# x turned in blocks by VectorE and through DRAM, and the carried sum added on GpSimd, in a Mamba-2 layer

## The reference

```
proj = layernorm(x) @ in_proj_w.T          # gate 8192 | hBC 8192 + 2*8*128 | dt 128
hBC  = silu(causal_conv4(hBC) + conv_b)    # hs (128 heads x 64), B, C (8 groups x 128)
dt   = clip(softplus(dt + dt_bias))
xch  = hs * dt                             # per token and head
Y_diag = (C B^T * L) xch                   # inside a chunk of 128 tokens
states = B^T (decay * xch)                 # one per chunk
new_states = states carried from chunk to chunk
Y_off  = C prev_state * exp(A_cum)         # from the chunks before
y    = Y_diag + Y_off + hs * D
g    = y * silu(gate); normed over groups of 1024 features; * norm_w
x    = x + g @ out_proj_w.T
```

## Time and profile before

| | us |
|---|---|
| median of 3 runs | 1605.14 |
| lowest and highest run | 1604.95, 1605.45 |
| the profiled execution, its span | 1605.0 |
| PE busy | 1583.5 (99%) |
| DVE busy | 1264.2 (79%) |
| ACT busy | 1163.1 (72%) |
| POOL busy | 700.7 (44%) |

### The profile page before, as it was taken

One profiled execution on the slowest core, in us unless ns is written; L12 is line 12 of the kernel. 1 busy time (PEld: TensorE's weight loads), 2 busy tenths in 40 slices (PEclk: granted clock), 3 DMA queues, 4 the chain that ended last, 5 costly groups with the idle time before them and its releaser, 6 DMA issues.

```text
span 1605.0 us, 26714 instructions
## 1 busy us (share of the span) xinstructions
PE 1583.5 (99%) x9576; PEld 1346.1 (84%) x9576; DVE 1264.2 (79%) x1984; ACT 1163.1 (72%) x2027; POOL 700.7 (44%) x535
## 2 busy tenths in 40 slices
PE   7899999999999999999999999999999999999998
PEld 5688888888888888888888888888888888888887
DVE  6687777877778777887778877787877878788787
ACT  5887667776777677777687766777677767777753
POOL 2155444453444454354453544445344445435550
PEclk9999999999999999999999999999999999999999
DMA  4542322332323233332232232233232323223211
GB/s 151 192 145 86 122 89 83 112 112 73 112 97 114 73 109 95 98 106 92 99 108 97 86 122 89 83 112 112 73 112 99 113 73 109 99 92 112 93 44 53
DMA packets 86916, 162.37 MB, mean 101 GB/s; under 512 B 23040, under 2 KB 39424, under 8 KB 86528
## 3 DMA queue, kind: packets, MB, share of 16 engines
q1 hardware_dynamic: 86784, 160.66, 30.8%
HBM read 154.84 MB, written 5.77 MB: 100 GB/s over the span
## 4 chain that ended last, share of the span: by engine, by line
PE 97%; DVE 1%; ACT 1%; issue 0%; DMA 0%; SPq 0%; DVEq 0%; ACTq 0%
PE g_bank L778 10%; PE g_bank L780 9%; PE g_bank L779 9%; PE d_bank L797 7%; PE x_bank L778 7%; PE x_bank L780 7%; PE x_bank L779 7%; PE head_bank L786 5%; PE head_bank L804 5%; PE x_bank L836 4%; PE x_bank L837 4%; PE x_bank L835 4%; PE d_bank L837 4%; PE d_bank L835 4%; PE d_bank L836 4%; PE head_bank L812 3%
## 5 line engine op out<-in xcount | busy, mean ns | idle before, releaser
L1448 POOL TENSOR_TENSOR w_low<-raw,w_high 128x512 fp32r<-128x512 f32 x139 | 179.8, 1294 | 553.5 <-ACT w_high L1011 553.5
L1199 DVE SCALAR_TENSOR_TENSOR hs<-x_bank,cols,hs 128x1022 f32<-128x1022 f32 x189 | 241.6, 1278 | 129.7 <-ACT hs L1033 127.5
L1021 ACT ACTIVATE scores<-scores,tables 128x128 f32<-128x128 f32 x1024 | 312.4, 391 | 0.0
L1462 POOL TENSOR_TENSOR y<-y,gate 128x512 f32<-128x512 f32 x128 | 185.4, 1467 | 198.8 <-DVE y L1268 198.8
L1033 ACT ACTIVATE hs<-x_bank,cols 128x1024 f32<-128x1024 f32 x63 | 75.9, 1204 | 269.9 <-PE x_bank L780 269.9
L778 PE MATMUL g_bank<-x_high,w_high 128*128 128x512 f32 x624 | 250.8, 402 | 0.0
L779 PE MATMUL g_bank<-x_low,w_high 128*128 128x512 f32 x624 | 243.2, 390 | 0.0
L780 PE MATMUL g_bank<-x_high,w_low 128*128 128x512 f32 x624 | 243.1, 390 | 0.0
L778 PE MATMUL x_bank<-x_high,w_high 128*128 128x512 f32 x504 | 196.3, 390 | 0.1
L780 PE MATMUL x_bank<-x_high,w_low 128*128 128x512 f32 x504 | 196.1, 389 | 0.0
L779 PE MATMUL x_bank<-x_low,w_high 128*128 128x512 f32 x504 | 196.1, 389 | 0.0
(11 more groups left out here) (211 smaller groups left out, 3433.3 us busy)
## 6 DMA issues: line engine op xcount, KB each, us to landing
scores<-sums_dram SPq DMA_DIRECT2D x128, 512.0 KB, 4.8
raw<-w_in SPq DMA_DIRECT2D x144, 256.0 KB, 2.9
grown_rows<-grown_dram SPq DMA_DIRECT2D x256, 96.0 KB, 2.8
out_raw<-w_out SPq DMA_DIRECT2D x64, 256.0 KB, 3.4
mixed<-x SPq DMA_DIRECT2D x8, 256.0 KB, 5.1
out<-mixed SPq DMA_DIRECT2D x8, 256.0 KB, 2.0
table_dram<-table SPq DMA_DIRECT2D x2, 768.0 KB, 5.3
tables<-table_dram SPq DMA_DIRECT2D x30, 48.0 KB, 2.7
```

The lines of the kernel that those rows point to most:

```text
L1021: op = s.activation(at, at, ACT.Relu, bias=col[:, r, c:c + 1], scale=-1.0)
L1199: v.scalar_tensor_tensor(out=hs[:, q % 2, :, i:], in0=x_bank[:, :, 0:SEQ - i], scalar=cols[:, q, TAPS - 1 - i:TAPS - i], in1=hs[:, q % 2, ...
L1448: pool.tensor_tensor(w_low[:, slot], raw[:, slot], w_high[:, slot].bitcast(F32), ALU.subtract)\
L1462: pool.tensor_tensor(y[:, b], y[:, b], gate[:, q % 2, b], ALU.mult).then_inc(y_ready, 1)
```

## The change

Hs of a unit is no longer turned by TensorE (only that of the very first unit is). DVE transposes it in blocks of 32x32 (`turn_blocks`), SP stores the blocks to DRAM (`store_blocks`, one DMA of 512 KB) and loads them back in four DMAs of 128 KB, each to 32 partitions, in pieces of 1 KB (`load_heads`), so that tokens lie on the partitions. `to_heads` reads this buffer instead of `head_bank`, with dt doubled in the tables (four kinds instead of three), and it has moved behind the two scores. `add_carry` has moved from DVE to GpSimd, ahead of each `gated`. In SP's queue the store stands before `load_grown` and the loads behind it. `states` now waits for `carry_scaled` of the unit before, as `turn_hs` did. The split bias has no buffers of its own any more and uses parts of x_low and x_high, so its copy waits until all projections are done.

The diff, without signatures and allocations:

```diff
             def table_of(i):
-                s.activation(table[:, b, :, kind].rearrange("p g (h c) -> p c g h", c=CHUNKS), ..., ACT.Copy)
+                if kind == 0:
+                    twice = table[:, b, :, 0:2].rearrange("p g k (h z c) -> p z c g (k h)", z=2, c=CHUNKS)
+                    s.activation(twice[:, 0], src, ACT.Copy)
+                    s.activation(twice[:, 1], src, ACT.Copy).then_inc(table_ready, 1)
...
+            def store_blocks(k):
+                sp.wait_ge(blocks_ready, k)
+                reached(sp, heads_in, 16 * QUARTERS * (k - 2))
+                sp.dma_start(blocks_dram[k % 2], blocks[:].rearrange("p j n f -> p (j n f)"))\
+                  .then_inc(blocks_stored, 16)
+
+            def load_heads(k):
+                sp.wait_ge(blocks_stored, 16 * k)
+                turned_blocks = blocks_dram[k % 2].rearrange("(q t) (j n) -> j t q n", t=BLOCK, j=QUARTERS)
+                for i in range(QUARTERS):
+                    sp.dma_start(blocks[i * BLOCK:(i + 1) * BLOCK].rearrange("p q n f -> p q (n f)"),
+                                 turned_blocks[i]).then_inc(heads_in, 16)
...
                     if ahead:
+                        store_blocks(ahead[2])
                         for b in range(BATCH):
                             load_grown(ahead[2], b)
+                        load_heads(ahead[2])
...
             def states(k, b):
                 pe.wait_ge(xdecay_ready, BATCH * k + b + 1)
+                reached(pe, carry_scaled, BATCH * (k - 1) + b + 1)
...
-                    if ahead:
-                        for b in range(BATCH):
-                            turn_hs(k + 1, (j + 1) % 2, b)
...
+            def turn_blocks(k, i):
+                v.wait_ge(hs_ready, k + 1)
+                reached(v, blocks_stored, 16 * (k - 1))
+                v.transpose(blocks[:], hs[:, i].rearrange("p b (c j t) -> p j (b c) t", j=QUARTERS, t=BLOCK))\
+                 .then_inc(blocks_ready, 1)
...
             def to_heads(g, q, k, b):
...
+                else:
+                    v.wait_ge(heads_in, 16 * QUARTERS * k)
+                    v.tensor_tensor(xdt[:, b].rearrange("p c r (h f) -> p (r h) c f", f=BLOCK),
+                                    blocks[:, :, CHUNKS * b:CHUNKS * (b + 1)],
+                                    dt_of(b, q).unsqueeze(3).to_broadcast([P, QUARTERS, CHUNKS, BLOCK]), ALU.mult)\
+                     .then_inc(xdt_ready, 1)
...
-                    for b in range(BATCH):
-                        to_heads(g, j, k, b)
+                    if k == 0:
+                        for b in range(BATCH):
+                            to_heads(g, j, k, b)
...
                     if scores_here:
                         score(g, j, k, 1)
+                    if k > 0:
+                        for b in range(BATCH):
+                            to_heads(g, j, k, b)
...
                         skip(j, k)
+                        turn_blocks(k + 1, (j + 1) % 2)
                         for b in range(BATCH):
                             carry_part(k, b)
-                        for b in range(BATCH):
-                            add_carry(k, b)
...
         @block.gpsimd
+            def add_carry(k, b):
+                u = BATCH * k + b
+                pool.wait_ge(skip_added, k + 1)
+                pool.wait_ge(carry_scaled, u + 1)
+                pool.tensor_tensor(y[:, b, P:], y[:, b, P:], grown[:, b].rearrange("p c l -> p (c l)"), ALU.add)\
+                    .then_inc(y_sum, 1)
...
                     for b in range(BATCH):
+                        add_carry(k, b)
                         gated(j, k, b)
...
-        bias_high, bias_low = sb("bias_high", [P, HID], F32R), sb("bias_low", [P, HID], F32R)
+        bias_high, bias_low = x_low[:, 1, 0], x_high[:, 1, 0]
...
+                        s.wait_ge(projected, BATCH * TILES)
                         s.activation(bias_high[:], bias_row, ACT.Copy).then_inc(bias_high_ready, 1)
```

More of the change, by code:

```diff
@@ L21 @@
 PAIR = P // HEAD_DIM
+BLOCK = 32
+KINDS = 4
+QUARTERS = P // BLOCK
 GH = HEADS // GROUPS
@@ L158, in prologue @@
         sums, grown = big("head_sums"), big("head_grown")
-        table = sb("table", [P, BATCH, 2 * GROUPS, 3, GH // 2 * CHUNKS])
+        table = sb("table", [P, BATCH, 2 * GROUPS, KINDS, GH // 2 * CHUNKS])
         la, lb = sb("la", [P, ER, HID]), sb("lb", [P, ER, HID])
@@ L400, in table_of @@
                 s.wait_ge(table_turned, i + 1)
-                s.activation(table[:, b, :, kind].rearrange("p g (h c) -> p c g h", c=CHUNKS),
-                             bank[4 + i % 2].rearrange("p (c g h) -> p c g h", c=CHUNKS, g=2 * GROUPS),
-                             ACT.Copy).then_inc(table_ready, 1)
+                src = bank[4 + i % 2].rearrange("p (c g h) -> p c g h", c=CHUNKS, g=2 * GROUPS)
+                if kind == 0:
[3 more added lines that the diff above has]
+                else:
+                    s.activation(table[:, b, :, 1 + kind].rearrange("p g (h c) -> p c g h", c=CHUNKS), src, ACT.Copy)\
+                        .then_inc(table_ready, 1)
             def first_tables(b):
@@ L600, in mixer @@
     TB = BATCH * CHUNKS
-    DT, SUMS, DECAY = range(3)
+    SUMS, DECAY = 2, 3
     with ExitStack() as ctx:
@@ L612, in mixer @@
         out_raw = sb("out_raw", [P, 2, HID])
+        blocks = sb("blocks", [P, QUARTERS, BATCH * CHUNKS, BLOCK])
         xdt = sb("xdt", [P, BATCH, CHUNKS, PAIR, HEAD_DIM])
@@ L655, in mixer @@
                              "last_low_ready", "norm_bias_ready", "bias_high_ready", "bias_low_ready"))
+        blocks_ready, blocks_stored, heads_in = (sem(n) for n in ("blocks_ready", "blocks_stored", "heads_in"))
         block = ctx.enter_context(nc.Block())
@@ L662, in table_of, with dt_of @@
             return tables[:, b, q // HALF, kind, PAIR * (q % HALF):PAIR * (q % HALF + 1)]
+        def dt_of(b, q):
+            twice = tables[:, b, q // HALF, 0:2].rearrange("p k h c -> p (k h) c")
+            return twice[:, QUARTERS * (q % HALF):QUARTERS * (q % HALF + 1)]
         (first_sync, first_stores, first_dense, first_gpsimd, first_tensor, first_scalar, first_vector,
@@ L806, in carry, with turn_first @@
                 mm.then_inc(carried, 1)
-            def turn_hs(k, s, b):
-                pe.wait_ge(hs_ready, k + 1)
-                reached(pe, carry_scaled, BATCH * (k - 1) + b + 1)
+            def turn_first(b):
+                pe.wait_ge(hs_ready, 1)
                 for c in range(CHUNKS):
-                    mm = pe.transpose(head_bank[b][:, c * P:(c + 1) * P], hs[:, s, b, c * P:(c + 1) * P], ident[:])
+                    mm = pe.transpose(head_bank[b][:, c * P:(c + 1) * P], hs[:, 0, b, c * P:(c + 1) * P], ident[:])
                 mm.then_inc(turned, 1)
@@ L895, in body @@
                                 pe.wait_ge(bc_ready, 1)
-                                turn_hs(0, 0, 0)
-                                turn_hs(0, 0, 1)
+                                turn_first(0)
+                                turn_first(1)
                     if j == 0:
@@ L1273, in to_heads @@
                     v.wait_ge(tables_in[b][q // HALF], 16 * (g + 1))
-                v.wait_ge(turned, BATCH * k + b + 1)
                 reached(v, diag_done, BATCH * (k - 1) + b + 1)
                 reached(v, xdecay_ready, BATCH * (k - 1) + b + 1)
[L1277 to L1280, removed]
+                if k == 0:
+                    v.wait_ge(turned, b + 1)
+                    col = dt_of(b, q)[:, 0::QUARTERS // PAIR].rearrange("p r c -> p c r")
+                    v.tensor_tensor(xdt[:, b], head_bank[b].rearrange("p (c r d) -> p c r d", c=CHUNKS, r=PAIR),
+                                    col.unsqueeze(3).to_broadcast([P, CHUNKS, PAIR, HEAD_DIM]), ALU.mult)\
+                     .then_inc(xdt_ready, 1)
+                else:
+                    v.wait_ge(heads_in, 16 * QUARTERS * k)
+                    v.tensor_tensor(xdt[:, b].rearrange("p c r (h f) -> p (r h) c f", f=BLOCK),
+                                    blocks[:, :, CHUNKS * b:CHUNKS * (b + 1)],
+                                    dt_of(b, q).unsqueeze(3).to_broadcast([P, QUARTERS, CHUNKS, BLOCK]), ALU.mult)\
+                     .then_inc(xdt_ready, 1)
             def keep_bc(g, src):
```

10 lines of the change are left out of this document (6 added, 4 removed).

## The result

The changed kernel takes 1776.47 us (median of 4 runs, 1775.44 to 1779.06), the kernel before 1605.3 on the same chip: a ratio of 1.1065, 95% interval 1.1049 to 1.1081. It is slower by 171 us. The prediction had the direction, and 1667 us, 109 too little; 1776 lies outside its range.

A forecast was written before the change was run, and what follows sets the result against it. It took TensorE (PE) as the bound, busy 1583.5 of 1605.0 us. 1605.0 - 54.8 (products removed) + 113.8 (stalls) + 3 (smaller parts) = 1667 us, range 1590 to 1712.

The forecast's parts named there:

- What is removed: TensorE: the eight identity products of a unit, 0.87 us, go in 63 units, -54.8 us.
- turn_blocks: DVE: the added block transpose taken as a single pass over 1024 elements, 1.27 us, bounds half and double.
- GpSimd's part: GpSimd after carry_part: add_carry about 1.01 us each, second y_sum 3.99 us after carry_part starts.
- SP's queue: SP: last heads' load issued 6.88 us after carry_part starts, landing after 2.8; next to_heads 9.70 after carry_part starts.
- the rival of a queue that backs up: SP's queue: issues of 0.9 us or a landing of 4 give 1718 us; chance of over 1700, 0.12.
- c + 11: Next to_heads 11 us after carry_part starts (c, counted from PE starting states); a group then loses 19.5 us.
- The late tap: DVE, units 1 to 3: first tap waits behind y_low and normed_out (2.07 us for three), at most 3.5 us late.
- The prediction's own rule: Per unit: next stall is to_heads' start against PE's start of states, plus 3.17 us; 13.1 us a group.
- GpSimd and DVE in turns: SBUF reads: xdecay and y_low exclude each other, so both xdecay take 3.84 us from to_heads, 1.75 without y_low between.
- the rival in which both xdecay get through ahead of y_low: GpSimd: price 1.75 us for 3.17, total 1596; chance 0.28, shared with a short trip, under 1603.
- c = the larger of s + 9.77 and 10.08 + d: Start of carry_part after PE starts states, in us: s is the unit's stall, d the lateness of DVE's first tap.
- The rival on the other side: SP's queue to landing: shorter trip gives 1624 or 1597 us; 0.10 for 1603 to 1635, 0.28 under 1603, shared.

The follow-up runs named there:

- e9: Changed kernel with heads' loads ahead of the grown loads, to_heads ahead of the second score, normed_out at the end of carry_part: 1584.0 us, 0.9865 of the kernel before.
- e11: Changed kernel with normed_out alone moved to the end of carry_part: 1724.4 us.
- e3: Changed kernel with load_heads ahead of load_grown in SP's queue: 1632.5 us.

## Why the prediction was wrong

- **What is removed.** Right: in e9 units 4, 6 and 7 have 26.58, 22.94 and 21.84 where the prediction had 26.62, 22.95 and 21.93 without the products.
- **turn_blocks.** Right: 1.25 us, for the 1.27 taken from the earlier trace rows.
- **GpSimd's part.** Right where it runs alone: 1.01 to 1.02 us for the sum, taken as 1.01 from the earlier trace rows; the second y_sum 4.03 us after carry_part in units 0, 1 and 7, 3.99 predicted. In units 2 and 3 it comes after 4.7 and 4.9 in the mean, for there the second sum mostly runs beside a score of DVE and takes 2.0 us (2.03 at 370.15).
- **SP's queue.** The order and the issues were right (6.76 for 6.88). The step "A load of 96 KB lands after 2.8 in the median; I take that for 128 KB" was mis-sized: the last of the four took 4.06 in unit 2. For the to_heads of units 0 to 4 the whole way from carry_part takes 10.2 to 11.3 us in the mean over the groups, not 9.70. That was the rival of a queue that backs up: "at c + 11 a group loses 19.5, and the time is 1718". The Trainium skill's figure for 128 KB, which the prediction put beside it (DMA: Bandwidth & Descriptors, § Anatomy of one DMA), is lower still, 2.3 us, and was measured on transfers that GpSimd issues, where SP issues these; the trace has 2.9 in the median.
- **The late tap.** This is the step that failed most: "in units 1, 2, 3 behind `normed_out`, 2.07 for three of them, held 0.7 by the second xdecay". It counted the meeting with the second xdecay, and not that `normed_out`, once late, runs beside GpSimd's splits and squares as well. The three took 5.7, so that from to_heads to tap 1 units 2 and 3 take 8.7 us, where 5.9 had been reckoned and e11, with normed_out moved, takes 3.0. e11 is at 1724.4, 52 us less; that is the worth of all of normed_out in this place, not of the collision alone.
- **The two together.** The prediction's own rule can be run again with what the trace shows (means of groups 1 to 6). It had 13.1 us a group. With the real trips ahead of units 0 to 4 (10.6, 10.6, 10.3, 11.4, 10.8 us) it gives 18.3; with the real way from to_heads to tap 1 as well (5.9 us in unit 1, 8.7 in units 2 and 3) 24.7; with carry_part 2.4 us late in unit 4 as well, 27.1. A group of the trace takes 210.6 us against 183.6 of PE's own work, so it loses 27.0. Of the 13.9 us missing in a group the trip has 5.2, the collision 6.4 and the wait for PE at its lower clock 2.4. That is 84 of the 109 us; the other 25 stand in the first and the last group and were not split. The split is worked out, not measured, but for e11: with its own trips and no normed_out ahead of the tap the rule gives 16.2 a group for it, and its trace has 18.6, carry_part in some groups again late behind PE in units 0, 2 and 3.
- **GpSimd and DVE in turns.** Right: xdecay takes 1.45 us in the mean (0.87 before), and in unit 2 the states of the two batches start 2.0 and 3.8 us after to_heads, as reckoned (3.84 for the second), so the rival in which both xdecay get through ahead of y_low is out. Units 5 and 6 stall 1.6 us, as predicted.
- **The clock.** Not in the prediction. In units 2 and 3 it did not have to be; in unit 4 it is the 2.4 us a group above, which the rule "c = the larger of s + 9.77 and 10.08 + d" leaves out.
- **The rival on the other side** ("The trip is short enough, so faster") gets its condition with the loads ahead of the grown loads, but not its result: in e3 DVE waits for the trip only 10 us in all, and the kernel is still 27 us slower than before. The same rival had 1553 us for no stall at all, and the best that was reached is 1584.

Why the last landing is 4.06 and not 2.9 was not tested. Two loads of 256 KB (raw and out_raw) go out right behind the four, which would fit, but no run moved them.

## What to carry to other kernels

When an engine's input comes late, everything behind it in that engine's written order is late as well: list that queue and see which work of another engine it will now run beside, above all DVE and GpSimd work that both read SBUF. Look at what a transfer is queued behind before its length: here 144 us hung on the order of two statements of SP, and about 3 on the trip itself. And when several limits lie close together, judge reorderings in combination: on top of e3, two steps that gained 1 and lost 7 us alone gained 48 together. A control that leaves the total where it was can hide a gain and a loss, so read it unit by unit.

## What the runs showed of the hardware

- A pause of 3.5 us in TensorE's work was followed by 5 us at 1.2 GHz (granted clock 0.50), in which twelve products took 3.43 us instead of 1.50. 24 products that nothing uses, set into the pauses, kept the clock at 1.00 in units 2 and 3 of group 1 and changed the whole time by under 1 us; unit 4 got 1.3 us shorter and others longer.
- One DVE instruction of 128x512 with its inputs in SBUF took 0.7 us alone, 1.5 us in the mean against GpSimd's sum and gate (e9) and 1.9 us against its weight splits and squares.
- A 32x32 block transpose of 128x1024 fp32 on DVE took 1.25 us, as long as a tap or skip over as many elements (1.27).
- A store of 512 KB from SBUF to DRAM landed 2.6 us after its issue in the median, a load of 128 KB to 32 partitions in pieces of 1 KB after 2.9.
